# A GNN stack on one core: edge attribute sums of layer 3 with the one-hot as the fixed operand of the matmul

## The reference

```python
i_idx_e = jnp.concatenate([edge_index[0], edge_index[1]])
g2 = jnp.concatenate([g, g], axis=0)            # g = edge_attr_64 @ W_edge.T
...
alpha_e = segment_softmax(e_e, i_idx_e, N)
x_from_edges = scatter_mean(alpha_e[:, None] * g2, i_idx_e, N)
```

## Time and profile before

| | us |
|---|---|
| median of 3 runs | 3198.73 |
| range of the runs | 3195.99 to 3198.73 |
| span of the profiled execution | 3214.4 |
| edge loop in it, first to last matmul of line 2459 | 2620.5 to 2847.8 |
| from there to the first operation after the stage | 2847.8 to 2854.8 |

### The profile page before, as it was taken

The page is one execution under the profiler, slowest core; times in us unless marked ns, Lnnn a source line. Parts: engine busy times, 40 slices in busy tenths (PEclk is TensorE's granted clock), DMA queues, the critical chain, the costliest instruction groups (busy, mean ns, idle before and its releaser), DMA issues. The chain is left out here.

```text
span 3214.4 us, 41518 instructions
## 1 busy us (share of the span) xinstructions
PE 1763.8 (55%) x11979; PEld 1235.9 (38%) x11979; DVE 2154.6 (67%) x4708; ACT 788.4 (25%) x2131; POOL 1494.4 (46%) x1520
## 2 busy tenths in 40 slices
PE   5333222356666643776268220196117789975995
PEld 4222111234444432675157210043112258853653
DVE  8788666477777854887878250003779966657986
ACT  0111111123333321333100010001018845533342
POOL 0777777577777761455756667500500025520000
PEclk9999999976776676888589655598559999977997
DMA  8666656488888879985078200283856636625761
GB/s 276 183 190 189 191 150 178 110 222 239 241 241 238 239 182 83 211 228 141 1 166 193 40 2 3 76 304 131 334 229 250 230 91 129 129 45 140 201 188 44
DMA packets 703255, 535.18 MB, mean 166 GB/s; under 512 B 396620, under 2 KB 653196, under 8 KB 691286
## 3 DMA queue, kind: packets, MB, share of 16 engines
q1 hardware_dynamic: 640980, 414.56, 50.4%
q0 software_dynamic: 58752, 102.49, 9.0%
q10 hardware_dynamic: 3312, 15.48, 1.2%
HBM read 371.29 MB, written 161.06 MB: 166 GB/s over the span
## 5 line engine op out<-in xcount | busy, mean ns | idle before, releaser
L669 POOL DMA_INDIRECT adjacency<-gm_slot,slot_tmp x440 | 457.3, 1039 | 374.2 <-DMA adjacency<-gm_slot,slot_tmp 211.9
L1445 POOL DMA_INDIRECT table<-pay_own,stage x432 | 414.8, 960 | 234.6 <-issue 122.8
L1445 POOL DMA_INDIRECT table<-q,stage x424 | 409.7, 966 | 130.1 <-issue 118.3
L1407 PE MATMUL banks<-acc,work 128*128 128x26 bf16 (+1 forms) x856 | 82.3, 226 | 437.8 <-DVE work L1401 437.3
L1673 PE MATMUL banks<-pool,both 128*128 x1320 | 254.2, 359 | 118.2 <-ACT pay_own L1683 64.1
L2412 POOL TENSOR_TENSOR pool<-pool,raw 128x260 f32<-128x260 f32 x110 | 115.1, 1047 | 400.4 <-DMA pool<-table 291.0
L1379 DVE TENSOR_SCALAR work<-acc,pidx 128x512 bf16<-128x512 bf16 x214 | 81.1, 379 | 251.2 <-DMA acc<-low_rows_by_src 133.1
L1407 PEld LDWEIGHTS banks<-acc,work 128*128 128x128 bf16 x856 | 47.5, 111 | 498.0 <-DVE work L1401 494.3
L1673 PEld LDWEIGHTS banks<-pool,both 128*128 128x128 bf16 x1320 | 156.9, 119 | 193.3 <-issue 138.7
L2019 PE MATMUL banks<-work,pool 128*128 128x512 f32 (+1 forms) x350 | 137.1, 555 | 149.7 <-DMA work<-adjacency 149.7
L1397 ACT CAST work<-banks 128x104 bf16<-128x104 f32 x214 | 59.2, 277 | 608.7 <-PE banks L1389 539.3
(11 more groups left out here) (504 smaller groups left out, 4719.6 us busy)
## 6 DMA issues: line engine op xcount, KB each, us to landing
work<-adjacency SPq DMA_DIRECT2D x75, 1600.0 KB, 7.0
acc<-table SPq DMA_DIRECT2D x110, 332.0 KB, 4.8
q<-table SPq DMA_DIRECT2D x110, 256.0 KB, 3.9
pool<-table SPq DMA_DIRECT2D x220, 128.0 KB, 2.4
adjacency<-slots SPq DMA_DIRECT2D x65, 392.0 KB
work<-adjacency SPq DMA_DIRECT2D x25, 832.0 KB, 5.3
work<-adjacency SPq DMA_DIRECT2D x25, 768.0 KB, 5.0
adjacency<-slots ACTq DMA_DIRECT2D x11, 1320.0 KB
```

Source lines behind the costliest of these rows:

```text
L669: nc.gpsimd.indirect_dma_start(adjacency, bass.IndirectOffsetOnAxis(ap=pair_at[:, t:t + 1], axis=0), pair_n[:, t:t + 1], None).then_inc(co ...
L1407: last = nc.tensor.matmul(table[:, 0:j + 1, :], oh_keys[n % 3][:, j, :], hi16[n % 4][:, j:j + 1, :].to_broadcast([P, j + 1, NH]), start=Fa ...
L1445: nc.gpsimd.indirect_dma_start(to, bass.IndirectOffsetOnAxis(ap=stage[n % 4][:, j:j + 1], axis=0), pay[n % 4][:, j, 0:width], None).then_i ...
```

## The change

The two operands of the edge matmul change places. The one-hot (128 x 128) becomes the fixed operand and the 65 weighted attributes stream, so the sums come out with nodes on the 128 partitions and attributes as columns. Each block still owns its 128 columns of the banks, of which 65 are used. With nodes on the partitions already, the turn back falls away: `turned`, the 25 transposes, VectorE's four last copies and the two semaphores go, and a helper `keep_bank` copies 4 blocks x 65 columns out of each bank straight into `edge_sum`, four banks on ScalarE and three on VectorE.

```diff
--- before.py
+++ after.py
@@ -2390,9 +2390,11 @@
             ORD = ("src", "dst")
             s_ld = {o: [sem(f"attributes_{o}_loaded{k}") for k in range(RING)] for o in ORD}
             s_oh, s_we, s_pd = ({o: sem(f"{k}_{o}") for o in ORD} for k in ("marked", "edges_weighted", "edges_summed"))
-            s_o, s_tb = sem("edge_sums_kept"), sem("edge_sums_turned_back")
-            turned = work[0:A + 1, 0:NPAD]
             groups = T // G
+
+            def keep_bank(copy, c):
+                n = min(MAIN, NB - c * MAIN)
+                copy(edge_sum[:, c * MAIN:c * MAIN + n, :], ps[c][:, 0:n * P].rearrange("p (b c) -> p b c", c=P)[:, :, 0:A + 1])
 
             with nc.Block() as block:
                 @block.sync
@@ -2425,9 +2427,8 @@
                         last.then_inc(s_we["src"], 1)
                     act.wait_ge(s_pd["src"], groups)
                     act.wait_ge(s_pd["dst"], groups)
-                    for q in range(0, 7, 2):
-                        n = min(512, NPAD - q * 512)
-                        nc.scalar.copy(turned[:, q * 512:q * 512 + n], ps[q][0:A + 1, 0:n]).then_inc(s_o, 1)
+                    for c in range(0, 7, 2):
+                        keep_bank(nc.scalar.copy, c)
 
                 @block.vector
                 def _(v):
@@ -2440,13 +2441,8 @@
                                                     ALU.is_equal).then_inc(s_oh[o], 1)
                     v.wait_ge(s_pd["src"], groups)
                     v.wait_ge(s_pd["dst"], groups)
-                    for q in range(1, 7, 2):
-                        nc.vector.tensor_copy(turned[:, q * 512:(q + 1) * 512], ps[q][0:A + 1, :]).then_inc(s_o, 1)
-                    for c in range(4):
-                        n = min(7, NB - 7 * c)
-                        v.wait_ge(s_tb, c + 1)
-                        nc.vector.tensor_copy(edge_sum[:, 7 * c:7 * c + n, :],
-                                              ps[c][:, 0:n * (A + 1)].rearrange("p (b c) -> p b c", b=n))
+                    for c in range(1, 7, 2):
+                        keep_bank(nc.vector.tensor_copy, c)
 
                 @block.tensor
                 def _(pe):
@@ -2456,16 +2452,9 @@
                             pe.wait_ge(s_oh[o], n + 1)
                             pe.wait_ge(s_we[o], n + 1)
                             for j in range(G):
-                                last = nc.tensor.matmul(banks[0:A + 1, bass.ds(blocks[j] * P, P)], weighted[o][:, n % 2, j, :],
-                                                        marked[o][n % 2][:, j, :], start=False, stop=True, skip_group_check=True)
+                                last = nc.tensor.matmul(banks[:, bass.ds(blocks[j] * P, A + 1)], marked[o][n % 2][:, j, :],
+                                                        weighted[o][:, n % 2, j, :], start=False, stop=True, skip_group_check=True)
                             last.then_inc(s_pd[o], 1)
-                    pe.wait_ge(s_o, 7)
-                    for b in range(NB):
-                        c, j = b // 7, b % 7
-                        last = nc.tensor.transpose(ps[c][:, j * (A + 1):(j + 1) * (A + 1)], turned[:, b * P:(b + 1) * P],
-                                                   ident[0:A + 1, 0:A + 1])
-                        if j == 6 or b == NB - 1:
-                            last.then_inc(s_tb, 1)
 
         with nc.Block() as block:
             @block.vector
```

## The result

The median went from 3198.55 us (3195.99 to 3198.73 over 4 runs) to 3343.94 us (3338.67 to 3344.19 over 4 runs), a ratio of 1.0453 with a 95% interval of 1.0438 to 1.0468. The forecast was 3194 us, with 3187 to 3200 as its range.

The account below looks back on a forecast made before the run. The prediction took TensorE's sequencer to bound the edge loop. Savings of 0 (loop) + 0.4 (last group) + 4.35 (copies) = 4.75 us took the median from 3198.73 to 3194.0 us, range 3187 to 3200.

Parts of the forecast that it names:

- What bounds the kernel: Layer 3's edge loop: TensorE's sequencer sets the pace, 0.99 us a group plus 0.04 irregular; the array has room.
- Matmul of 65 columns: Edge loop's matmul: eight records take 0.60 us instead of 0.85, sequencer's 0.99 us stays, so value 0 for 220 groups.
- loads that don't hide: Edge loop, slower: 128-column loads stand open at clock 0.50; all eight open cost 213 us more, 3407 us; chance 0.05.
- The other rivals: Edge loop, faster: array the bound after all, 3120 us, chance 0.04; irregular part goes with array's lag, 3185 us, 0.08.
- the irregular 0.04 us: Edge loop: part of the mean 1.03 us a group above 0.99; at best it goes, 9 us gained.
- End of the last group: Last group of the edge loop: last record starts sooner and streams half as long, 0.4 us saved, bounds 0 and 0.5.
- Copies and turn back: Behind the edge loop: seven copies side by side, 1.1 us in place of 5.46, 4.35 us saved, bounds 4.0 and 4.5.
- may be lower in the loop at no cost: Expected sign in the edge loop: the granted clock may fall, while line 465 still comes every 2.06 us a pair.
- more than 2.1 us a pair (loads): Sign of being wrong: a pair of edge-loop groups takes more than 2.1 us, pointing to the loads.

## Why the prediction was wrong

**What bounds the kernel: right.** The sequencer set 1.03 us a group, and the main reading from the earlier trace rows was borne out by the run with fixed block numbers: 32.7 us less of loop, where 22 to 35 us were expected. The pieces that the prediction added up to 0.99 us were not taken apart one by one. The Trainium skill's share of LDWEIGHTS ("Trainium Kernel Development and Optimization", section "Performance Expectations") would have pointed to the array at 82%; here the measurement decides for the sequencer.

**Matmul of 65 columns: this step failed.** It said 0.60 us for eight records at clock 1.00 and at most 0.93 at 0.50, both under 1.03, and so put the loop's change at 0. The runs show 8 x 0.111 = 0.89 at 1.00 (which still hides) and 1.71 at 0.50 (which does not): (1.71 - 1.03) x 220 = 149.6 us, the loop's 148.4. The rows taken for it were those of transposes. They have the columns of the new matmuls, f32 with 128 fixed and 65 streamed (on 65 partitions, not 128), but one record where the matmul has two, and a record costs half as much: at most 0.117 us at 0.50 where the matmul's is 0.213. The shape was matched and the kind of operation was not. The trace before had rows of the right kind too. The loads of the earlier trace rows belong to f32 matmuls with 128 columns fixed and 64 streamed, at clock 0.50:

```profile
2868.88 0.69 PE L907 MATMUL banks<-wedgeT,xt 64*128 64x64 f32 x2
```

The second of its two records starts 0.27 us after the first. The same distance is 0.20 us or more in 10 of the 19 matmuls of line 518 that ran at clock 0.50 (f32, 128 fixed, 32 streamed), and 0.07 to 0.13 in the others. The larger ones are well above the 0.129 us at which the array becomes the bound. They come one matmul at a time, so they are no clean price, but they were nearer than the transposes and should have widened the bound.

The prediction also set aside a sentence of the Trainium skill ("TensorE: Matmul & The Clock Gate", section "LDWEIGHTS (loading the stationary operand)"): a load costs its columns over 1.2 GHz, which makes 107 ns for 128 columns. At clock 1.00 the runs agree with it for f32 matmuls (0.11 us a record); the disagreement that the prediction saw came from transposes. At 0.50 they don't: 0.213 us, twice that. An estimate from the page's figure, 8 x 0.107 = 0.86 us a group, would have shown no loss at the slow clock either.

**The clock.** The prediction allowed for 0.50 but took it as harmless, from the earlier trace rows, where the sequencer kept its pace at the start. It did not ask whether the clock would rise again. Before, it did, 4.2 us into the loop, although records were then as far apart as in the changed kernel (1.76 us a group, 1.71 after). So the exchange changed a record's price at neither clock; it changed whether the clock rises. The loss needs two parts: loads of 128 f32 columns that take longer than the group's 1.03 us at 0.50, and a narrow stream that leaves the clock where it is. Remove either (64 fixed, or 128 streamed) or enter at 1.00, and the 148 us are gone. Why the clock rises with one stream and not with the other, no run shows.

**The rival "loads that don't hide"** named the place (0.129 us a record as the limit) and the condition (clock 0.50). Its price of 0.25 us a record, 213 us, was taken from loads back to back; the record is 0.213 and the loss 148. Its chance of 0.05 was too low, since the transposes were held against it. Its first reason, that a less busy array lets the clock fall in the loop, is not what happened: the clock was at 0.50 at the entry, as before, and did not rise. The other rivals did not occur: the array was not the bound before, and the irregular 0.04 us stayed even in the loops with both operands narrow, where the array stands for a third of the time.

**End of the last group.** In the kernel with the ten matmuls, the last group ran at 1.10 us, not shorter than 1.08: the 0.4 us were not there, as the load sets the record. The lower bound of 0 was right.

**Copies and turn back: right.** 4.36 us less from last matmul to next operation, against 4.35 worked out; in every kernel with the new end the stretch is 2.65 us. That the two agree so closely is in part luck: in the other kernels with the old end the stretch was 6.25 to 6.56 us, so the saving can be as little as 3.6 us.

The granted clock "may be lower in the loop at no cost" was the sentence on what would show it; "more than 2.1 us a pair (loads)" was the one that did, with 3.41.

## What to carry to other kernels

Price a matmul from rows of the same kind and type as well as the same shape; a transpose is no stand-in for an f32 matmul. Before making a stream narrower, work out what the loop costs at clock 0.50 and whether it would rise from there: a loop that is fast only at full clock can stay slow to its end after one stall. Here a record cost what the wider of its two operands cost, whichever side that was on; but with the wide one streaming the clock rose, and with the wide one fixed and the narrow one streaming it did not.

## What the hardware showed unexpectedly

The same loop ran at two paces, depending on the clock at which it entered: 1.03 us a group at 1.00 (held for 223 us) and 1.71 at 0.50 (held for 370 us). A stall of 3.8 us was enough to change over, and ten matmuls ahead of the loop enough to avoid it. The Trainium skill ("TensorE: Matmul & The Clock Gate", "What's actually happening") says that the slow clock is the default and that activity releases it; the runs agree in that the clock fell to 0.50 during each stall of TensorE ahead of or in the loop (3.8 to 5.0 us) or within 1.4 us of its end, and differ in that a loop whose pace the loads set, recorded as busy for 370.00 of 370 us, did not release it.

With 65 columns streamed, an f32 matmul's record with 128 fixed columns starts 0.213 us after the one before at clock 0.50 and 0.11 us at 1.00, and with 64 fixed columns 0.11 us at 0.50. So the load's price goes with the fixed columns and with the clock. With 65 fixed and 128 streamed the distances are the same 0.213 and 0.109 us. Why the clock stayed at 0.50 with the filler of 256 bf16 columns a group, and rose with 4 x 63 more columns of f32 in two records each, the runs don't tell.
